# The first batch's xT is loaded by two requests of two row tiles each instead of one request of four

## The chip, the cores and the metric

The kernel runs on one core of one Trainium2 chip. The metric is the device time of one execution in microseconds (us). The kernel before takes 541.18 us (median of 3 runs, 540.99 to 541.9).

## What is computed

There are 16 independent batches, each a graph of 512 nodes with 256 features: x is 512 x 256 and adj is 512 x 512, all float32. Each batch goes through two residual blocks, a one-layer graph product and then a three-layer one:

```python
x = layernorm(x + adj @ (x @ W0 + b0) / rowsum(adj))
s = relu(adj @ (x @ W1) + b1)
s = relu(adj @ (s @ W2) + b2)
s = adj @ (s @ W3) + b3
out = layernorm(x + s)
```

No batch depends on another.

## The kernel before, in words

T = 4 row tiles of 128 nodes make up a batch, and KF = 2 tiles of 128 features. Every matrix that enters a product is split into a high and a low part (`_hi`, `_lo`): ScalarE (ACT) makes the high part with a copy, VectorE (DVE) or GpSimd (POOL) subtracts it from the full value for the low part. Each product is then three matmul passes on TensorE (PE): high times high, high times low, low times high (`three_passes`). The eight products of a batch are named p0 to p7: p0 is x @ W0 (it reads xT, x with its features on the partitions), p1 is adj @ h, which gives the first block's v1, p2 is the first product of the second block (it reads x1, the normalized v1), and so on.

The engines run queues written out by hand, and meet at counting semaphores. Batch 0 is `FIRST`, batch 1 is `second`; both have a start of their own, and from batch 2 on a loop does three batches a turn. The work of one batch is interleaved with that of the batch before and the one after.

Loads are issued by two engines, SyncE (SP) and ScalarE, each with a queue of its own: in the DMA rows q1 is SP's and q10 is ScalarE's. A load of a 128-partition tile reaches all 16 DMA engines, and each engine takes 8 partition rows of it. At the start of the kernel ScalarE issues, in this order, w0 (256 KB), the low half of batch 0's transposed adjacency (512 KB), batch 1's xT into the tile `y`, the low half of batch 1's adjacency into `adj_rows`, and batch 1's x into the tile `v2` (`v` in the rows). SP issues batch 0's xT (L220), the high half of batch 0's adjacency (L222), the biases b03 (L223, 256 KB), batch 0's x (L224), the high half of batch 1's adjacency (L225), W1 to W3 (L226) and the small biases (L227). Each of those without a size is 512 KB.

What reads them at the start, in queue order:

- ScalarE: `split_xT(FIRST, 0)` and `split_xT(FIRST, 1)` (high parts of row tiles 0, 1 and of 2, 3; L506, shown as L487), then the high parts of adjacency tiles 0 and 1, h tiles 0 and 1, adjacency tile 2, h tile 2, adjacency tile 3, h tile 3, and then batch 1's work.
- VectorE: w0's two parts, `split_xT(FIRST, 0)` and `(FIRST, 1)` (low parts), the low part of adjacency tile 0, h's low parts, then `norm1(FIRST)`.
- GpSimd: the low parts of adjacency tiles 1, 2 and 3 (L932), then `add_b0(FIRST)` (L914), which adds the bias to x_raw and gives xb; VectorE's v1 (L766) needs xb.
- TensorE: 18 warm-up matmuls on zeros, then `p0_first` (L308), which takes row tiles 0 to 3 in order. Tiles 0 and 1 need only the first half of xT, tiles 2 and 3 the second. Then come `p1_first` (which takes adjacency tile by adjacency tile for the first two outputs, and then outputs 2 and 3), `p0(second)`, and `p2_first`, whose four steps each wait for a tile of x1.

`norm1(FIRST)` and the normalization on ScalarE (`normalize_first`, L565 and L567) lead from v1 to x1; the low parts of x1 come from `split_x1_tile` (L939 on GpSimd, L693 on VectorE).

Of the kernel before, what the change touches and what calls it, by code (L numbers as in the profile page):

```python
# [12 lines left out]
DMA = 16  # L13
# [6 lines left out]
def build(nc, xT, x, adjT, adj, w0, w123, b03, b12, out):  # L20
    NB = x.shape[0]
    T = x.shape[2]
# [6 lines left out]
    with ExitStack() as ctx:  # L29
        def sb(name, shape, dt):  # L30
            return ctx.enter_context(nc.sbuf_tensor(name, shape, dt))

        def sem(name):
            return ctx.enter_context(nc.semaphore(name))


        xT_raw = sb("xT_raw", [P, T, F], F32)
# [57 lines left out]
        w123_loaded = sem("w123_loaded")  # L95
        b03_loaded = sem("b03_loaded")
        b12_loaded = sem("b12_loaded")
        xT1_loaded = sem("xT1_loaded")
        xT_loaded = sem("xT_loaded")
        x_loaded = sem("x_loaded")  # L100
# [65 lines left out]
        def at(batch, per, n):  # L166

            turn, r = batch
            return turn * (RING * per) + (r * per + n)

        def out_of(batch):

            return v1 if batch is LAST else y
# [38 lines left out]
        @block.sync  # L212
        def _(sp):

            sp.sem_inc(stored, DMA)
            def half_of(half, n):
                return slice(half * n // 2, (half + 1) * n // 2)

            sp.sem_inc(rows_ready, 2 * T)
            sp.dma_start(xT_raw[:, :, :], xT[0]).then_inc(xT_loaded, DMA)  # L220
            high = half_of(1, T)
            sp.dma_start(adj_raw[:, high, :], adjT[0, :, high, :]).then_inc(adj_loaded[1], DMA)  # L222
            sp.dma_start(b03_all[:, :], b03).then_inc(b03_loaded, DMA)  # L223
            sp.dma_start(x_raw[:, :, :], x[0]).then_inc(x_loaded, DMA)  # L224
            sp.dma_start(adj1_raw[:, high, :], adjT[1, :, high, :]).then_inc(adj1_loaded[1], DMA)  # L225
            sp.dma_start(w_raw[:, 1:4, :, :], w123).then_inc(w123_loaded, DMA)  # L226
            sp.dma_start(b12_col[:, 0:2 * KF], b12).then_inc(b12_loaded, DMA)  # L227

            def load(i, adj_free, rows_free):

                for half in range(2):
                    tiles = half_of(half, T)
                    adj_free(half)
                    sp.dma_start(adj_raw[:, tiles, :], adjT[i, :, tiles, :]).then_inc(adj_loaded[half], DMA)
                sp.wait_ge(xT_split, i * 2)
                sp.dma_start(xT_raw[:, :, :], xT[i]).then_inc(xT_loaded, DMA)
                sp.wait_ge(xb_ready, i * T)
                sp.dma_start(x_raw[:, :, :], x[i]).then_inc(x_loaded, DMA)
                rows_free()
                sp.dma_start(adj_rows[:, :, :], adj[i]).then_inc(rows_loaded, DMA)  # L240

            def third_adj_free(half):
                for k in range(half * T // 2, (half + 1) * T // 2):
                    sp.wait_ge(adj_tile_split[0][k], 1)

            def third_rows_free():
                for k in range(T):
                    sp.wait_ge(adj_tile_split[1][k], 1)

            load(2, third_adj_free, third_rows_free)  # L250
            sp.wait_ge(y_ready, T)
            sp.dma_start(out[0], y[:, :, :]).then_inc(stored, DMA)
            with sp.Fori(3, NB) as i:
                load(i, lambda half: sp.wait_ge(adj_split, (i - 3) * T + (half + 1) * T // 2),
                     lambda: sp.wait_ge(rows_ready, i * T))

                sp.wait_ge(y_ready, (i - 1) * T)
                sp.dma_start(out[i - 2], y[:, :, :]).then_inc(stored, DMA)
            sp.wait_ge(y_ready, (NB - 1) * T)
            sp.dma_start(out[NB - 2], y[:, :, :]).then_inc(stored, DMA)  # L260

            for j in range(T):
                sp.wait_ge(y_ready, (NB - 1) * T + j + 1)
                sp.dma_start(out[NB - 1, :, j, :], out_of(LAST)[:, j, :]).then_inc(stored, DMA)
            sp.wait_ge(stored, (1 + NB - 1 + T) * DMA)
# [219 lines left out]
        def _(act):  # L485
            def copy_hi(dst, src):
                return act.activation(dst, src, ACT.Copy)  # L487
# [6 lines left out]
            def split_xT(nxt, half):  # L494

                tiles = slice(half * T // 2, (half + 1) * T // 2)
                if nxt is second:
                    act.wait_ge(xT1_loaded, DMA)
                elif nxt is FIRST:
                    act.wait_ge(xT_loaded, DMA)  # L500
                else:
                    act.wait_ge(xT_loaded, at(nxt, DMA, 0))
                if nxt is not FIRST:
                    act.wait_ge(p0_done, at(nxt, T, 0))
                raw = xT1_raw if nxt is second else xT_raw
                copy_hi(xT_hi[:, tiles, :], raw[:, tiles, :]).then_inc(xT_hi_ready, 1)  # L506
# [105 lines left out]
            def step(new, last=False, ahead=True):  # L612
                old, nxt = before(new), before(new, -1)
                x3(old, 0)
                x3(old, 1)
                g(new, 0)
                if not last:
                    split_xT(nxt, 0)
                    split_xT(nxt, 1)
                g(new, 1)  # L620
                s3(old)
                x2(new, 0)
                x2(new, 1)
                if not last:
                    norm2(old, nxt=nxt)
                    h(nxt)
                    s2(new)
                    norm1(nxt, before(new, -2) if ahead else None)

            low = slice(0, T // 2)  # L630
# [5 lines left out]
            act.dma_start(adj1_raw[:, low, :], adjT[1, :, low, :]).then_inc(adj1_loaded[0], DMA)  # L636
            act.dma_start(x1_raw[:, :, :], x[1]).then_inc(x1_loaded, DMA)
            split_xT(FIRST, 0)
            split_xT(FIRST, 1)
            split_adj(FIRST, 0)  # L640
# [392 lines left out]
```

## Time and profile before

| | us |
|---|---|
| median of 3 runs | 541.18 (540.99 to 541.9) |
| the profiled execution | 541.69 |
| its span in the profile | 539.9 |
| PE busy | 531.2 (98% of the span) |
| DVE, ACT, POOL busy | 351.2, 312.4, 209.9 |

```profile
PE 531.2 (98%) x3829; PEld 496.8 (92%) x3829; DVE 351.2 (65%) x1059; ACT 312.4 (58%) x790; POOL 209.9 (39%) x227
...
PE   7899999999999999999999999999999999999996
...
PEclk9999999999999999999999999999999999999999
DMA  8530250703307051160602407043070612500002
```

These are the page's busy times and four of its lines in 40 slices of 13.5 us. A digit is the busy share of a slice in tenths. TensorE has a low digit only in the first slices and the last; the DMA engines are busiest in the first two. The span is the time between the first and the last instruction that the profile sees; the execution's own time lies 1.8 us above it.

### The profile page before, as it was taken

How to read it: one execution, taken by the hardware profiler on the slowest of the kernel's cores; microseconds unless marked ns; L12 is line 12 of the kernel's file. 1: busy time of each engine (PE TensorE's matmuls, PEld its weight loads, DVE VectorE, ACT ScalarE, POOL GpSimd, SP SyncE). 2: the span in 40 equal slices, each digit the busy share in tenths (PEclk: the TensorE clock that was granted, in tenths of full speed). 3: DMA queues.
4: the chain of work that ended last, by engine and by line, in shares of the span. 5: the costliest groups of instructions: out<-in, count | busy, mean ns of one | idle time of the engine just before them, and what ended most of it. 6: DMA issues, size and time to landing. Idle time of an engine off the chain costs nothing.

```text
span 539.9 us, 11045 instructions
## 1 busy us (share of the span) xinstructions
PE 531.2 (98%) x3829; PEld 496.8 (92%) x3829; DVE 351.2 (65%) x1059; ACT 312.4 (58%) x790; POOL 209.9 (39%) x227
## 2 busy tenths in 40 slices
PE   7899999999999999999999999999999999999996
PEld 7798989999899998989989899998999989899896
DVE  5684766747567475765757667485675757657546
ACT  5756655475665656655566655746655566554542
POOL 2667127081450906317072360904408063271100
PEclk9999999999999999999999999999999999999999
DMA  8530250703307051160602407043070612500002
GB/s 324 202 118 0 70 206 1 272 2 128 145 0 272 0 188 84 46 226 0 255 17 72 200 0 272 0 145 127 12 260 0 210 63 60 215 0 40 2 1 78
DMA packets 14566, 58.23 MB, mean 108 GB/s; under 512 B 1744, under 2 KB 2256, under 8 KB 12752
## 3 DMA queue, kind: packets, MB, share of 16 engines
q1 hardware_dynamic: 13824, 55.58, 28.2%
q10 hardware_dynamic: 720, 2.36, 1.2%
q8 instruction: 13, 0.21, 0.2%
q14 instruction: 9, 0.07, 0.0%
HBM read 49.55 MB, written 8.39 MB: 107 GB/s over the span
## 4 chain that ended last, share of the span: by engine, by line
PE 93%; DMA 2%; ACT 2%; DVE 1%; issue 0%; POOL 0%; SPq 0%; DVEq 0%; POOLq 0%
PE bank_a L186 16%; PE bank_a L187 16%; PE bank_a L188 16%; PE bank_b L186 15%; PE bank_b L188 14%; PE bank_b L187 14%; DMA x_raw<-in_x 2%; PE bank_b L278 1%; PE bank_b L279 1%; ACT x_hi L567 0%; ACT x L565 0%; DVE stats L820 0%; ACT adj_hi L487 0%; ACT std L607 0%; ACT h_hi L487 0%
## 5 line engine op out<-in xcount | busy, mean ns | idle before, releaser
L954 POOL TENSOR_TENSOR adj_lo<-adj_raw,adj_hi 128x512 fp32r<-128x512 f32 x56 | 70.7, 1296 | 261.8 <-ACT adj_hi L487 261.8
L693 DVE TENSOR_TENSOR x_lo<-bank_a,x_hi 128x512 fp32r<-128x512 f32 x62 | 42.8, 691 | 66.7 <-ACT bank_a L588 66.7
L186 PE MATMUL bank_b<-h_hi,adj_hi 128*128 128x256 f32 (+1 forms) x256 | 71.1, 278 | 0.4 <-POOL adj_lo L932 0.3
L555 ACT ACTIVATE std<-moments,eps_col 128x1 f32<-128x1 f32 x64 | 18.9, 295 | 90.5 <-DVE moments L790 90.5
L187 PE MATMUL bank_b<-h_lo,adj_hi 128*128 128x256 f32 (+1 forms) x256 | 70.8, 277 | 0.0
L188 PE MATMUL bank_b<-h_hi,adj_lo 128*128 128x256 f32 (+1 forms) x256 | 70.8, 276 | 0.0
L188 PE MATMUL bank_b<-s_hi,adj_lo 128*128 128x256 f32 x232 | 64.1, 276 | 0.0
L186 PE MATMUL bank_b<-s_hi,adj_hi 128*128 128x256 f32 x232 | 64.0, 276 | 0.0
L187 PE MATMUL bank_b<-s_lo,adj_hi 128*128 128x256 f32 x232 | 64.0, 276 | 0.0
L586 ACT ACTIVATE x_hi<-bank_a,b_col 128x512 fp32r<-128x512 f32 x62 | 42.3, 682 | 20.5 <-PE bank_a L188 19.6
L920 POOL TENSOR_TENSOR x1b<-x,b_all 128x256 f32<-128x256 f32 x64 | 46.0, 750 | 17.2 <-DVE x L777 17.2
L186 PE MATMUL bank_a<-adj_hi,s_hi 128*128 128x512 f32 x128 | 50.2, 392 | 0.0
L187 PE MATMUL bank_a<-adj_lo,s_hi 128*128 128x512 f32 x128 | 50.0, 391 | 0.0
L188 PE MATMUL bank_a<-adj_hi,s_lo 128*128 128x512 f32 x128 | 49.8, 389 | 0.0
L607 ACT ACTIVATE std<-moments,eps_col 128x1 f32<-128x1 f32 x64 | 18.9, 295 | 51.9 <-DVE moments L832 51.9
L186 PEld LDWEIGHTS bank_b<-h_hi,adj_hi 128*128 128x128 f32 x256 | 48.1, 188 | 0.9 <-issue 0.8
L188 PEld LDWEIGHTS bank_b<-h_hi,adj_lo 128*128 128x128 f32 x256 | 48.1, 188 | 0.0
L187 PEld LDWEIGHTS bank_b<-h_lo,adj_hi 128*128 128x128 f32 x256 | 48.1, 188 | 0.0
L693 DVE TENSOR_TENSOR g_lo<-bank_a,g_hi 128x512 fp32r<-128x512 f32 x30 | 20.7, 691 | 40.8 <-ACT g_hi L487 40.8
L186 PE MATMUL bank_a<-adj_hi,x_hi 128*128 128x512 f32 x120 | 46.7, 389 | 0.0
L187 PE MATMUL bank_a<-adj_lo,x_hi 128*128 128x512 f32 x120 | 46.7, 389 | 0.0
L188 PE MATMUL bank_a<-adj_hi,x_lo 128*128 128x512 f32 x120 | 46.7, 389 | 0.0
(150 smaller groups left out, 1721.2 us busy)
## 6 DMA issues: line engine op xcount, KB each, us to landing
adj_raw<-in_adjT SPq DMA_DIRECT2D x29, 512.0 KB, 5.5
adj_rows<-in_adj SPq DMA_DIRECT2D x14, 1024.0 KB, 9.4
xT_raw<-in_xT SPq DMA_DIRECT2D x15, 512.0 KB, 6.3
x_raw<-in_x SPq DMA_DIRECT2D x15, 512.0 KB, 7.3
out_y<-y SPq DMA_DIRECT2D x15, 512.0 KB, 2.9
w_raw<-in_w SPq DMA_DIRECT2D x1, 768.0 KB, 13.1
adj_raw<-in_adjT ACTq DMA_DIRECT2D x1, 512.0 KB, 6.1
y<-in_xT ACTq DMA_DIRECT2D x1, 512.0 KB, 7.9
```

The costliest lines, as they stand in the source:

```text
L186: pe.matmul(acc, st[0], mv[0], start=start, stop=False)
L187: pe.matmul(acc, st[0], mv[1], start=False, stop=False)
L188: return pe.matmul(acc, st[1], mv[0], start=False, stop=stop)
L278: pe.matmul(bank[j][:, 0:2 * F], hi, w_both[:, n, k, :, :], start=True, stop=False)
L279: mm = pe.matmul(bank[j][:, 0:F], lo, mv[0], start=False, stop=False)
L555: act.activation(std1[:, j:j + 1], moments1[:, j, 1:2], ACT.Sqrt, bias=eps_col[:, :]).then_inc(std1_ready, 1)
L586: act.activation(hi[:, f, :], bank[:, :], ACT.Relu, bias=bias[:, f:f + 1])
L607: act.activation(std2[:, j:j + 1], moments2[:, j, 1:2], ACT.Sqrt, bias=eps_col[:, :]).then_inc(std2_ready, 1)
L693: return dve.tensor_tensor(lo, full, hi.bitcast(F32), ALU.subtract)
L920: pool.tensor_tensor(x1b[:, slot(batch), j, :], x1[:, j, :], b3_all[:, :], ALU.add).then_inc(x1b_ready, 1)
L954: pool.tensor_tensor(adj_lo[:, s, k, :], adj_raw[:, k, :], adj_hi[:, s, k, :].bitcast(F32), ALU.subtract).then_inc(adj_split, 1)
```

## The change

The first request (xT of batch 0, all four row tiles, one semaphore) becomes two requests of two row tiles each, with a semaphore for each half. Each half is 256 KB; a partition row of it is 2 KB instead of 4 KB. ScalarE's `split_xT(FIRST, half)` waits for its own half. The semaphore of the later batches' xT starts one load lower. ScalarE and SP are the only queues whose text changes.

```diff
+        xT0_loaded = [sem(f"xT0_half{n}_loaded") for n in range(2)]
...
-            sp.dma_start(xT_raw[:, :, :], xT[0]).then_inc(xT_loaded, DMA)
-            high = half_of(1, T)
+            low, high = half_of(0, T), half_of(1, T)
+            sp.dma_start(xT_raw[:, low, :], xT[0, :, low, :]).then_inc(xT0_loaded[0], DMA)
+            sp.dma_start(xT_raw[:, high, :], xT[0, :, high, :]).then_inc(xT0_loaded[1], DMA)
...
                 elif nxt is FIRST:
-                    act.wait_ge(xT_loaded, DMA)
+                    act.wait_ge(xT0_loaded[half], DMA)
                 else:
-                    act.wait_ge(xT_loaded, at(nxt, DMA, 0))
+                    act.wait_ge(xT_loaded, at(nxt, DMA, -DMA))
```

On SyncE, at the start of the program, the kernel before has these requests (`b_all` is b03, `adj_rows` holds batch 1's adjacency here):

```order
L220 DMA xT_raw<-in_xT 128x1024
L222 DMA adj_raw<-in_adjT 128x1024
L223 DMA b_all<-in_b 128x512
L224 DMA x_raw<-in_x 128x1024
L225 DMA adj_rows<-in_adjT 128x1024
```

The changed kernel has these in the same place:

```order
L222 DMA xT_raw<-in_xT 128x512
L223 DMA xT_raw<-in_xT 128x512
L224 DMA adj_raw<-in_adjT 128x1024
L225 DMA b_all<-in_b 128x512
L226 DMA x_raw<-in_x 128x1024
L227 DMA adj_rows<-in_adjT 128x1024
```

One request of 1024 columns has become two of 512, and everything behind it is one request further back; x_raw is now the fifth in SyncE's queue. ScalarE's queue keeps its order: its two copies of xT stand ahead of the copies of the adjacency, the first waiting for the first half and the second for the second.

## Rows read from the trace of the kernel before

**Rows 1.** Busy time in stretches: us, PE, PEld, DVE, ACT, POOL, clock, DMA, GB/s
```profile
50.00:100.00 50.00, 50.00 (x392) 47.98 (x391) 33.77 (x103) 30.60 (x81) 19.87 (x23) 1.00 0.27 92
...
450.00:500.00 50.00, 50.00 (x376) 47.37 (x375) 35.43 (x113) 27.42 (x76) 15.12 (x17) 1.00 0.23 85
```

**Rows 2.** What PE waited for, whole span: us in total, times, longest
```profile
PE bank_b L314 <- ACT xT_hi L487: 1.1, 1, 1.1
PE bank_b L186 <- DVE x_lo L693: 1.0, 1, 1.0
```

**Rows 3.** The chain that ended last, in order of time: start us, us, what
```profile
2.27 11.12 DMA x_raw<-in_x
...
24.56 0.75 POOL x_lo L939
25.36 0.50 PE bank_b L186
```

**Rows 4.** The timeline's DMA requests: start us, us that issuing took, queue, line
```profile
0.88 0.39 SPq L220 DMA_DIRECT2D xT_raw<-in_xT  x1
1.17 0.45 ACTq L632 DMA_DIRECT2D adj_raw<-in_adjT  x1
1.32 0.43 SPq L222 DMA_DIRECT2D adj_raw<-in_adjT  x1
...
2.27 1.11 SPq L224 DMA_DIRECT2D x_raw<-in_x  x1
...
3.15 0.56 ACTq L637 DMA_DIRECT2D v<-in_x  x1
```

**Rows 5.** DMA issues before 3.25 us: count, KB, us from issue to landing
```profile
xT_raw<-in_xT SPq DMA_DIRECT2D x1, 512.0 KB, 4.6
adj_raw<-in_adjT ACTq DMA_DIRECT2D x1, 512.0 KB, 6.1
adj_raw<-in_adjT SPq DMA_DIRECT2D x1, 512.0 KB, 7.6
...
x_raw<-in_x SPq DMA_DIRECT2D x1, 512.0 KB, 11.1
v<-in_x ACTq DMA_DIRECT2D x1, 512.0 KB, 11.2
```

**Rows 6.** DMA queues, 3.75 to 4.5 us: packets, MB, share of 16 engines
```profile
q1 hardware_dynamic: 75, 0.31, 100.0%
q10 hardware_dynamic: 3, 0.00, 0.8%
```

**Rows 7.** DMA queues, 4.5 to 5 us
```profile
q1 hardware_dynamic: 43, 0.12, 59.2%
q10 hardware_dynamic: 24, 0.10, 47.7%
```

**Rows 8.** DMA queues, 5.5 to 6 us
```profile
q10 hardware_dynamic: 33, 0.14, 74.3%
q1 hardware_dynamic: 14, 0.06, 27.8%
```

**Rows 9.** DMA queues, 8 to 10 us, where SP's queue carries b03
```profile
q10 hardware_dynamic: 150, 0.55, 67.1%
q1 hardware_dynamic: 145, 0.27, 34.6%
```

**Rows 10.** DMA queues, 0 to 13.4 us
```profile
q10 hardware_dynamic: 701, 2.35, 49.8%
```

**Rows 11.** DMA queues, 12.8 to 13.4 us
```profile
q10 hardware_dynamic: 30, 0.12, 50.6%
```

**Rows 12.** ScalarE in the timeline: start us, us, line, what [idle before <- releaser]
```profile
5.51 1.15 ACT L487 ACTIVATE xT_hi<-xT_raw 128x512 fp32r<-128x512 f32 x2 [2.37 <-DMA xT_raw<-in_xT]
7.28 1.16 ACT L487 ACTIVATE adj_hi<-adj_raw 128x512 fp32r<-128x512 f32 x2 [0.61 <-DMA adj_raw<-in_adjT]
```

**Rows 13.** GpSimd in the timeline
```profile
8.51 3.79 POOL L932 TENSOR_TENSOR adj_lo<-adj_raw,adj_hi 128x512 fp32r<-128x512 f32 x3 [8.06 <-ACT adj_hi L487]
13.53 2.15 POOL L914 TENSOR_TENSOR xb<-x_raw,b_all 128x256 f32<-128x256 f32 x3 [1.23 <-DMA x_raw<-in_x]
```

**Rows 14.** TensorE in the timeline: `p1_first` at its fourth adjacency tile
```profile
12.45 0.36 PE L186 MATMUL bank_b<-h_hi,adj_hi 128*128 128x258 f32 x1 [0.29 <-POOL adj_lo L932]
```

## The prediction

> **What bounds the kernel now.** I read the busy times by stretch first. From 50 to 500 us TensorE is busy in all 50.00 us of each 50 us stretch [rows 1] (the first and the last of nine stretches). Whatever happens there, nothing that this change touches can be late or early. What is left is the start, and a change there moves the end one for one: TensorE's work behind the start has no idle time to take up a delay or to fill with a gain.
>
> The list of TensorE's waits comes next. Two in the start matter: 1.1 us before the first p0 matmul, for the copy of xT, and 1.0 us in `p2_first`, for a low part of x1 [rows 2]. Only the first has to do with xT; the question is whether it is on the path, and the chain of waits says no. It runs over the load of x_raw, which is issued at 2.27 us and takes 11.12 us, up to 13.39; from there over xb, v1, the moments and ScalarE's normalization to the low part of x1's last tile (24.56 us, 0.75 us) and to the matmul at 25.36 us [rows 3]. GpSimd had been idle for 1.23 us when x_raw landed [rows 13]. TensorE waits again after its p0 and p1 work: a p0 that starts sooner only makes those later waits longer, as long as x_raw does not land sooner.
>
> The third view is the DMA queues, since x_raw's landing is a matter of their order. From 8 to 10 us they move 0.55 + 0.27 = 0.82 MB, 0.41 MB per us [rows 9], and that is the pace of the whole stretch up to x_raw: the landing is set by bytes ahead of it, not by its issue.
>
> **The first half and p0.** xT's request goes out at 0.88 us [rows 4] and lands 4.6 us later, at 5.48 [rows 5]; ScalarE copies from 5.51 on, after 2.37 us idle [rows 12]. Between 3.75 and 4.5 us the SP queue has the engines for itself [rows 6]: a half of 256 KB (0.262 MB) takes 0.262/0.41 = 0.64 us less than the whole, so it should land about 0.6 us sooner, near 4.9, and perhaps nearer 4.6. `p0_first` then starts about as much sooner. Worth on the path: 0, because x_raw's chain covers it. If this cover were gone it would be worth at most the 1.1 us of [rows 2].
>
> **The second half lands late.** The DMA queues show in which order packets are served. From 3.75 to 4.5 us xT alone is served, though the low adjacency half had been issued on ScalarE's queue at 1.17 us, before SP's next request at 1.32 [rows 4, 6]. Then the low adjacency half comes (24 packets from 4.5 to 5, xT's last 43 beside it) [rows 7], and only from about 5.7 does SP's second request begin (14 packets by 6.0) [rows 8]. So requests get served about in the order of issue over both queues, and SP's second request stands behind most of ScalarE's second one. From then on the queues alternate packet by packet: from 8 to 10 us SP's 2 KB rows of b03 get 145 packets against 150 packets of 4 KB, equal in number with half the bytes [rows 9]. In the changed kernel SP's second request is the second half of xT. It takes the high adjacency half's old place, moved 0.64 us forward by the shorter first half, and its 8 rows per engine alternate with 4 KB rows. A row of 4 KB takes 4096 x 16 / 0.41 MB per us = 0.16 us on an engine, one of 2 KB 0.08. The high adjacency half landed at 1.32 + 7.6 = 8.92 [rows 4, 5]; take off 0.64, and 8 x 0.08 = 0.64 for the shorter rows: about 7.6 us for xT's second half, 2.1 us after the whole xT lands now.
>
> What is queued behind that wait: ScalarE's second copy of xT, and behind it the copies of the adjacency, which start at 7.28 now [rows 12]. They would start at 7.6 plus one copy (1.15/2 = 0.6), near 8.2: 0.9 to 1.0 us late. GpSimd's three adjacency subtractions follow from 9.5 instead of 8.51 and end at 13.3 instead of 12.30 [rows 13]; TensorE's fourth adjacency step moves from 12.45 [rows 14] to about 13.4. All of this stays just ahead of xb, for GpSimd had 1.23 us of idle time before x_raw. Cost on the path: 0, with some 0.3 to 0.6 us of that cover left. If the second half came 0.5 us later than I say, this chain would take over from x_raw's.
>
> **x_raw lands later.** This is the term that counts. Bytes ahead of x_raw in SP's queue are the same as before, but there are 8 more rows per engine, and in packet-by-packet alternation each lets a row of ScalarE's queue pass. ScalarE's queue is nearly through when x_raw lands: batch 1's x (the `v` row) is issued at 3.15 and lands 11.2 later, at 14.35 [rows 4, 5], and five transfers of 128 rows and 16 small completion packets each are 720 packets, of which 701 were done by 13.4 [rows 10]. So the eight rows can let pass only what is left. Two readings of it: on the last engine 14.35 - 13.39 = 0.96 us of alternation, of which ScalarE's share is half, 0.48 us (3 rows of 0.16); over all engines the 0.12 MB after 12.8 us [rows 11], 0.29 us. (12.8 because xT's last packets went before 5.0 [rows 7] and its landing was at 5.48, so x_raw's last packets left about 0.5 us before 13.39.) I take 0.4 us, nearer to the last engine, which is the one that the semaphore waits for. Bounds: 0 if the second half is served right behind the first, since bytes and alternation then stay as they are up to there; 0.96 if all of batch 1's x and as much of SP's next load went ahead.
>
> **One more issue on SP.** Another request takes about 0.43 us to issue [rows 4], so x_raw's request starts at 2.7 instead of 2.27. It has over 9 us in the queue, with b03 ahead of it; cost 0. All other edits are semaphore counts; cost 0, as no instruction is added on the computing engines.
>
> **Sum.** 0 (p0 sooner) + 0 (adjacency later, covered) + 0.4 (x_raw) = +0.4 us. The profiled execution took 541.69 us, with 1.8 us around its span of 539.9, and would take 542.1; it lies 0.5 us above the median of the runs, 541.18, from which I forecast: 541.6 us.
>
> The Trainium skill, page "DMA: Bandwidth & Descriptors", section "Queues, rings and completion order", says that an engine drains a whole packet of some 9 to 17 descriptors from one queue before it turns to the other. Its rule would make the queues take turns by whole requests here. Rows 10 speak against it: when x_raw had landed, batch 1's x was nearly through, where by turns it would only be starting.
>
> **Rivals.**
> A, turns by whole requests. The place is the same, x_raw. Every request of SP is then followed by a whole one of ScalarE's, and the one request more lets all of batch 1's x (512 KB, 0.524/0.41 = 1.28 us) pass: +1.28, 542.5 us, slower. For it: the pure stretches of rows 6 and 7. Against it: rows 9, and the 701 packets of rows 10. This is the result of the page's rule named above.
>
> B, engines left idle: slower as well. The low adjacency half was issued at 1.17 us and had hardly a packet before 4.5 [rows 6, 7]. If that is no matter of order but the time at which its rows are there to be served, the shorter first half leaves the engines idle until then. This costs up to the whole 0.64 us, on top of the 0.4: +1.04, 542.2 us, and up to 542.7 if the later requests come at such intervals too. It decides from 1.08 us on. For it: the high adjacency half first shows at 5.7, 4 us after its issue, and the gaps between first packets are about 1.1 us. Against it: each first packet comes just where the other queue's request is nearly done, and no stretch after 3.75 us shows spare share.
>
> C, x_raw does not move: the halves are served back to back, or the engines' uneven pace swallows the three rows. 541.2 us. Also the case of a change that does what it says and is hidden at both ends.
>
> D, faster. The earlier p0 would have to reach the end, and that needs the 1.0 us wait in `p2_first` [rows 2] to fall with it. Only an earlier x_raw does that; were its chain gone, at most 1.1 us, 540.1. I see nothing for it but that the page attributes waits by inference.
>
> **How the numbers follow.** Forecast 0.52, A 0.04, B 0.20, C 0.21, D 0.03. Of this kernel 0.2% (1.08 us) is about what a measurement can tell from no change. Beyond it on the slow side lie A and half of B, with a little of the forecast's upper end (0.02): 0.16. On the fast side only D: 0.03. The rest, 0.81, is within. The range takes in the forecast (541.2 to 542.1 by its bounds), C with 0.3 us of scatter as in the runs of before, and B's first value: 540.9 to 542.7.
>
> **What the profile after would show.** Right: the first p0 matmul at least 0.5 us sooner; xT's second copy on ScalarE at 7.3 to 8 us, with TensorE waiting for it inside p0; the adjacency copies near 8.2; GpSimd's xb at 13.8 to 14.1, and still with idle time before it released by x_raw; the matmul of 25.36 [rows 3] at 25.7 to 25.9; from 50 us on no wait. Wrong: xT's second copy right after the first (then C), DMA shares that fall below full between 4 and 5 us (then B), xb later than 14.4 (A or B), or GpSimd's adjacency work ending after x_raw's landing, which would make the late second half itself the bound.

## The result and the profile after

The changed kernel takes 543.09 us (median of 6 runs, 542.82 to 543.29), the kernel before 541.13 in the same comparison (540.67 to 541.9). The ratio is 1.0033 with a 95% interval of 1.0024 to 1.0043: slower by 1.96 us, clear of noise. I had forecast 541.6, in a range up to 542.7. A second comparison gave 543.07 against 541.27, 1.0032 (1.0020 to 1.0045).

The profiled execution took 543.0 us with a span of 541.2; that of before took 541.69 with a span of 539.9. The spans are 1.3 us apart, less than the medians, because this execution of the kernel before was 0.5 us slower than its median. The chain of waits of the changed kernel (start, us, what) still runs over x_raw:

```profile
3.02 11.70 DMA x_raw<-in_x
...
25.89 0.76 POOL x_lo L941
26.64 0.04 issue
26.69 0.50 PE bank_b L187
```

Against [rows 3], x_raw lands at 14.72 instead of 13.39 and the matmul of 25.36 starts at 26.69: both 1.33 us later. The last matmul starts at 536.39 instead of 535.08, 1.31 us, so the end follows x_raw within 0.02 us. TensorE's waits over the whole span (us in total, times, longest) are:

```profile
PE bank_b L316 <- ACT xT_hi L489: 1.3, 2, 1.0
...
PE bank_b L187 <- DVE x_lo L695: 1.0, 1, 1.0
```

The first wait of [rows 2] has become two. p0 starts 0.6 us sooner, at 5.65 us, and then waits again for the second half of xT, which lands late. The DMA issues before 3.25 us of the changed kernel (count, KB, median us from issue to landing) show it together with x_raw's own landing:

```profile
xT_raw<-in_xT SPq DMA_DIRECT2D x2, 256.0 KB, 5.5
...
x_raw<-in_x SPq DMA_DIRECT2D x1, 512.0 KB, 11.7
```

The 5.5 is the middle of 4.0 and 7.0: the first half lands at 4.88, the second at 8.32, where the whole xT landed at 5.48 before. ScalarE and GpSimd in the timeline, against [rows 12, 13]:

```profile
4.88 0.63 ACT L489 ACTIVATE xT_hi<-xT_raw 128x512 fp32r<-128x512 f32 x1 [1.73 <-DMA xT_raw<-in_xT]
8.36 0.63 ACT L489 ACTIVATE xT_hi<-xT_raw 128x512 fp32r<-128x512 f32 x1 [2.85 <-DMA xT_raw<-in_xT]
8.89 1.14 ACT L489 ACTIVATE adj_hi<-adj_raw 128x512 fp32r<-128x512 f32 x2
```
```profile
10.11 4.01 POOL L934 TENSOR_TENSOR adj_lo<-adj_raw,adj_hi 128x512 fp32r<-128x512 f32 x3 [9.65 <-ACT adj_hi L489]
14.86 2.16 POOL L916 TENSOR_TENSOR xb<-x_raw,b_all 128x256 f32<-128x256 f32 x3 [0.74 <-DMA x_raw<-in_x]
```

The whole adjacency work is 1.6 to 1.8 us late, and still ends 0.74 us before xb may start. It is x_raw that ends the wait, as in the kernel before.

A part of x_raw's 1.33 us is seen in the DMA totals of the first 7 us, before and after:

```profile
DMA packets 523, 1.68 MB, mean 241 GB/s; under 512 B 48, under 2 KB 48, under 8 KB 523
```
```profile
DMA packets 580, 1.43 MB, mean 204 GB/s; under 512 B 49, under 2 KB 49, under 8 KB 580
```

More packets, and 0.25 MB less: at 0.41 MB per us that is 0.6 us lost for good. In these two profiles most of it lies between 5 and 7 us, where the two queues move 0.26 and then 0.33 MB in a microsecond, against 0.40 and 0.40 before (the sum of both rows in each stretch):

```profile
q10 hardware_dynamic: 49, 0.19, 72.2%
q1 hardware_dynamic: 34, 0.07, 17.8%
```
```profile
q10 hardware_dynamic: 83, 0.34, 89.3%
q1 hardware_dynamic: 16, 0.06, 14.0%
```

These are the rows of the stretch 5 to 6 us (packets, MB, share), the changed kernel first. A 4 KB row of ScalarE's queue (q10) takes longer here: 72.2% of 16 us over 49 packets is 0.24 us, against 0.17 before. From 7 us on both kernels run at 0.41 again.

The second profile of the changed kernel (e11) loses as much by 7 us, but from 4 us on. Its rows of 4 to 5 us:

```profile
q10 hardware_dynamic: 59, 0.24, 83.8%
q1 hardware_dynamic: 3, 0.00, 0.2%
```

The first half was through at about 4.0 us, and SyncE's queue (q1) is next served at 5.2. ScalarE's queue has the engines alone in between and moves 0.24 MB in this microsecond, where the kernel before moved 0.42 with both. The first profile has the same gap from 4.4 to 5.2 us. So a part of the loss comes before any row of the second half is served.

### The profile page after: what moved, and what is told of

It reads as the page before. It is cut to its first block, busy times and chain, and to the rows that moved or that the text cites. A ratio compares the mean times of both kernels' runs of the same rounds, so it can differ in the third digit from the quotient of the medians.

```text
span 541.2 us, 11046 instructions
## 1 busy us (share of the span) xinstructions
PE 532.2 (98%) x3829; PEld 497.7 (92%) x3829; DVE 351.2 (65%) x1059; ACT 312.4 (58%) x790; POOL 210.3 (39%) x227
## 4 chain that ended last, share of the span: by engine, by line
PE 92%; DVE 2%; DMA 2%; ACT 2%; issue 1%; SPq 0%; POOL 0%; DVEq 0%; POOLq 0%
PE bank_a L187 16%; PE bank_a L188 16%; PE bank_a L189 16%; PE bank_b L187 14%; PE bank_b L189 14%; PE bank_b L188 14%; DMA x_raw<-in_x 2%; PE bank_b L280 1%; PE bank_b L281 1%; ACT x_hi L569 0%; ACT x L567 0%; DVE x L779 0%; DVE stats L822 0%; ACT adj_hi L489 0%; ACT std L609 0%
```

## The experiments

All are compared with the kernel before on the same chips; its median (19 runs beside e1 to e4, 28 beside the others) was 541.27 to 541.30. "Landing" is x_raw's in the profiled execution, one for each kernel; a star marks where another load's chain set the time.

| kernel | median us | ratio, 95% interval | landing | MB by 7 us |
|---|---|---|---|---|
| before (two profiles) | 541.27, 541.14 | 0.9997 (0.9988 to 1.0006) | 13.39, 13.94 | 1.68, 1.66 |
| changed (two profiles) | 543.09, 543.07 | 1.0033, 1.0032 | 14.72, 14.62 | 1.43, 1.44 |
| e1 first copy waits for both halves | 544.16 | 1.0051 (1.0037 to 1.0065) | 14.9* | 1.43 |
| e2 halves by partitions | 544.47 | 1.0060 (1.0047 to 1.0074) | 15.9* | 1.41 |
| e3 tiny request second | 542.58 | 1.0025 (1.0016 to 1.0035) | 15.09 | 1.31 |
| e7 tiny request ahead of x_raw | 542.55 | 1.0022 (1.0013 to 1.0031) | 14.26 | 1.68 |
| e12 tiny request behind x_raw | 541.35 | 1.0002 (0.9993 to 1.0011) | 13.4 | 1.74 |
| e9 one request, 2 KB rows | 542.16 | 1.0018 (1.0009 to 1.0027) | 14.13 | 1.55 |
| e5 before, x1 last | 540.86 | 0.9993 (0.9984 to 1.0002) | 12.57 | 1.70 |
| e6 changed, x1 last | 542.15 | 1.0018 (1.0009 to 1.0027) | 13.51* | 1.45 |
| e8 second half on ScalarE's queue | 543.01 | 1.0030 (1.0018 to 1.0042) | 12.5* | 1.58 |
| e10 try at a faster kernel | 541.54 | 1.0005 (0.9996 to 1.0014) | 11.2* | 1.70 |

My theory after the result was that x_raw's landing sets the time and the DMA queues delay it, by rows that let the other queue pass and by a dead time at their start (a stretch in which the queues move less than they could). Its rival was that the late second half of xT itself sets the time.

**e1: both halves awaited by the first copy.**

```diff
-                    act.wait_ge(xT0_loaded[half], DMA)
+                    act.wait_ge(xT0_loaded[0], DMA)
+                    act.wait_ge(xT0_loaded[1], DMA)
```

> The changed kernel, but ScalarE's first copy of xT waits for both halves. The requests are the same. Theory Q (the DMA queues make x_raw land late, and nothing else counts): p0 starts near 9.0 instead of 5.65 us, x_raw still lands near 14.7, and the time is that of the changed kernel, 543.1 within 0.3. Theory W (the late second half holds up ScalarE's copies and the adjacency chain sets the time): that chain comes another half microsecond later, 543.6.

Neither number came: 544.16. With p0 at 9.29, the adjacency chain did take over, and by more than I had said. GpSimd's rows:

```profile
13.21 2.58 POOL L935 TENSOR_TENSOR adj_lo<-adj_raw,adj_hi 128x512 fp32r<-128x512 f32 x2 [0.99 <-ACT adj_hi L489]
15.74 1.90 POOL L917 TENSOR_TENSOR xb<-x_raw,b_all 128x256 f32<-128x256 f32 x2
```

xb starts with no idle time before it: its queue, not x_raw, was last. The adjacency copies wait in ScalarE's queue behind h's, and these for p0, whose matmuls ran at the lower rate after 3.9 us without work (last section). So the early start of the first half is worth about 1.1 us against this version; it only covers what the split itself makes late. In the changed kernel the late second half is not the bound: the work that it holds up still ends 0.74 us before xb may start (0.59 in e11).

**e2: two requests cut by partitions.**

```diff
-            sp.dma_start(xT_raw[:, low, :], xT[0, :, low, :]).then_inc(xT0_loaded[0], DMA)
-            sp.dma_start(xT_raw[:, high, :], xT[0, :, high, :]).then_inc(xT0_loaded[1], DMA)
+            sp.dma_start(xT_raw[0:P // 2, :, :], xT[0, 0:P // 2]).then_inc(xT0_loaded[0], DMA)
+            sp.dma_start(xT_raw[P // 2:P, :, :], xT[0, P // 2:P]).then_inc(xT0_loaded[1], DMA)
```

> xT comes in two requests, cut by partitions (64 partitions each, rows of 4 KB, 4 rows per engine and request), and ScalarE waits for both. The rows per engine are 8 as in the kernel before; only the request is one more. If it is the number of rows that counts (each lets a row of ScalarE's queue pass): x_raw at 13.4, 541.1 us. If it is the request itself (dead time of about 0.6 us between 5 and 7 us in the changed kernel): x_raw near 14.0, 541.8 us. If both halves of my sum are tied to the second request standing behind the low adjacency half: 542 to 543.

It was the slowest of all. With rows of 4 KB and no more rows than before, the queues moved only 0.3 MB per us from 6 to 8 us. xT's second part landed at 9.21 and x_raw at 15.9, later than any of the three cases expected. Since ScalarE waits for both parts as in e1, p0 and the adjacency chain were late too and set the time, so this run gives no price for one more request by itself. It does say that rows of full length do not save a cut load. That the place of the second part behind the other queue's load is what hurts in both cuts is likely, but not shown by this run.

**e3, e7, e12: one small request in three places.** In each, this line of the kernel before is moved up from the end of the first loads: in e3 behind xT's, in e7 ahead of x_raw's, in e12 behind it.

```diff
+            sp.dma_start(b12_col[:, 0:2 * KF], b12).then_inc(b12_loaded, DMA)
```

> The kernel before, with the small request b12 (128 rows of 16 bytes) moved from the end of SP's queue to the place right behind xT. One request and 8 rows per engine more stand ahead of x_raw, and next to no bytes. Row theory: the rows of the other queue that pass bring x_raw 0.3 to 0.5 us later, 541.5. Row and dead time together: x_raw at 14.3 to 14.7, 542.1 to 543.1. Byte theory (only bytes count): 541.1.

> The kernel before, with the small request b12 moved to the place right ahead of x_raw in SP's queue (fourth; in the run before it stood second and cost 1.4 us by the medians). Row theory: its 8 rows per engine let ScalarE's last rows pass, 0.3 to 0.5 us, 541.6. Dead time theory: an extra request costs 0.6 to 1.1 us only while the queues are starting up, so nothing of that shows here. If every request costs the same anywhere in the queue: 542.6 as for the second place.

> The kernel before, with the small request b12 moved to the place right behind x_raw in SP's queue. As second request it cost 1.4 us and right ahead of x_raw 1.3 (medians). Behind x_raw it can only delay later loads, which nothing waits for: 541.2 us, no change. If an additional request early in the program costs wherever it stands, 542 or more.

A load of 2 KB costs 1.3 us of the whole kernel when it stands ahead of x_raw, in either place, and nothing behind it. That refutes the byte theory. In e3 the small request is served in the queues' start, and the engines stand partly idle. The rows of 5 to 7 us:

```profile
q10 hardware_dynamic: 77, 0.27, 58.7%
q1 hardware_dynamic: 39, 0.00, 0.9%
```

That is 0.28 MB in 2 us, at a share of 60%, where the kernel before moves 0.80. But it is not only the start that is sensitive: e7 lost nothing by 7 us, and here is its stretch of 10 to 12 us, where the small request is served:

```profile
q10 hardware_dynamic: 160, 0.59, 79.4%
q1 hardware_dynamic: 164, 0.06, 10.5%
```

0.65 MB in 2 us instead of 0.82, in 324 packets: the two queues take turns packet by packet, and the 16 byte rows of the one do not leave their time to the other. This is 0.4 us. The rest of e7's 0.87 us by landings (14.26 against 13.39) fits rows of ScalarE's queue that went ahead of x_raw: batch 1's x, 0.96 us behind x_raw before, now lands at 3.04 + 10.4 = 13.4, ahead of it.

**e9: short rows without a second request.** The first batch's xT is stored as two halves in DRAM, and one request fetches both.

```diff
-            sp.dma_start(xT_raw[:, :, :], xT[0]).then_inc(xT_loaded, DMA)
+            sp.dma_start(xT_raw[:, :, :].rearrange("p (h t) f -> p h (t f)", h=2),
+                         xT0.rearrange("h p t f -> p h (t f)")).then_inc(xT_loaded, DMA)
```

> The kernel before, with batch 0's xT stored in DRAM as two halves one behind the other, so that its one request has 16 rows of 2 KB per engine instead of 8 of 4 KB; the bytes, the number of requests and the waits are those of before. This parts rows from requests. If the change's loss (1.3 us by x_raw's landing) comes with the rows that have to be served: the DMA queues fall behind between 5 and 7 us as in the changed kernel (1.43 MB by 7 us against 1.69) and x_raw lands near 14.5, 542.5 to 543 us. If it comes with the request and its place behind the low adjacency half: x_raw near 13.4 to 13.9, 541.3 us.

The median, 542.16, is 0.9 us above the kernel before, half of the change's 1.8 in these comparisons. By 7 us the queues have moved 1.55 MB, half of the shortfall. So the shorter rows alone, with the same bytes, the same request and the same wait, cost about half (0.5 to 1.5 us by the interval); the other half is left for the second request, by difference.

The loss does not come while the short rows are served. From 3.5 to 4 us they have the engines alone, at the full pace; from 5 to 6 us xT is through and ScalarE's 4 KB rows are served nearly alone (the rows of e9 in these two stretches):

```profile
q1 hardware_dynamic: 95, 0.19, 104.3%
```
```profile
q10 hardware_dynamic: 54, 0.22, 87.1%
q1 hardware_dynamic: 4, 0.02, 4.0%
```

This is the gap of e11 again, here from about 4.5 to 5.8 us: SyncE's first request is through, its second not yet served, and ScalarE's rows take 0.26 us each. The kernel before has such a gap too (4.9 to 5.6 us in the first profile, 4.6 to 5.4 in the second, e4). In its first profile ScalarE's queue kept the full pace in it, 0.20 MB from 5 to 5.5 us; in e4 it did not:

```profile
q10 hardware_dynamic: 34, 0.14, 99.3%
```

The gap is longer in the changed kernel (0.8 and 1.2 us) and in e9 (1.3) than in the kernel before (0.7 and 0.8). I read a part of the loss from this; no run changes the gap by itself.

**e5 and e6: batch 1's x moved out of ScalarE's queue**, in the kernel before and in the changed one.

```diff
-            act.dma_start(x1_raw[:, :, :], x[1]).then_inc(x1_loaded, DMA)
...
+            sp.dma_start(x1_raw[:, :, :], x[1]).then_inc(x1_loaded, DMA)
```

> The kernel before, with batch 1's x (512 KB, ScalarE's fifth request) moved to the end of SP's queue. In the first profile five of its eight rows per engine went ahead of x_raw. Row theory: x_raw lands 5 x 0.16 = 0.8 us sooner, and since the end follows x_raw one for one (+0.55 and +0.5 in the second profile of before), the time falls by 0.8 us, to 540.3. If another chain is right behind x_raw's, less of it is seen. If the number of requests in the first 7 us is what counts, x_raw gains less.

> The changed kernel with the same move of batch 1's x. Row theory: now all eight rows of it went ahead of x_raw, so x_raw gains 1.28 us, from 14.7 to 13.4, but GpSimd's adjacency work, which ended 0.74 us before x_raw's landing, then sets the time: a gain of 0.7, 542.4 us. If rows that pass were the whole of the change's cost, this kernel and the one before with the same move would be equal but for that chain; if the dead time is a part of its own, x_raw stays 0.6 us later than there.

x_raw gained 0.82 us in the one (12.57, by 0.8 as forecast) and 1.21 in the other. The difference, 0.39 us, looks like the term of 0.4 of my sum, but it hangs on which profiles are taken: against the second ones (13.94 and 14.62) the gains are 1.37 and 1.11, and the difference is -0.26. So the size of that term is not shown. Between e5 and e6, where these rows are out of the way, 0.94 us remain. 0.6 of them are the 0.25 MB by 7 us (1.70 and 1.45). The other 0.3 I can't place: it is smaller than the landing's own scatter. In e6 x_raw is no longer the bound; the chain runs over the high half of the adjacency:

```profile
1.80 8.79 DMA adj_raw<-in_adjT
...
11.32 2.24 POOL adj_lo L934 x2
13.56 0.26 issue
13.82 1.20 POOL xb L916
```

So the loads behind the split are late as well, and would cap what a better order could bring. By the median e5 is 0.4 us faster than before, half of what was expected, with an interval (0.9984 to 1.0002) that just includes no change. e6 came at 542.15, near the 542.4 expected.

**e8: the second half on ScalarE's queue**, ahead of the low adjacency half.

```diff
-            sp.dma_start(xT_raw[:, high, :], xT[0, :, high, :]).then_inc(xT0_loaded[1], DMA)
...
+            act.dma_start(xT_raw[:, T // 2:T, :], xT[0, :, T // 2:T, :]).then_inc(xT0_loaded[1], DMA)
```

> The changed kernel with the second half of xT issued by ScalarE, between w0 and the low adjacency half, instead of by SP. The number of requests and of rows is that of the changed kernel; the second half no longer stands behind the low adjacency half. Row theory: SP's queue has 8 rows fewer ahead of x_raw than in the changed kernel, so no row of ScalarE's passes in their place: x_raw near 13.4 if there is no dead time, near 14 to 14.4 if there is. Second half: lands near 5.5 to 6 instead of 8.3 us. Time 541.2 without, 541.8 to 542.2 with dead time.

The second half now landed at 1.17 + 4.3 = 5.5 us, and x_raw at 2.27 + 10.2 = 12.5. x_raw was sooner than I had expected (13.4 to 14.4), with 256 KB less ahead of it in SyncE's queue. In exchange the low adjacency half landed at 1.65 + 7.5 = 9.2 instead of 1.17 + 6.1 = 7.3, for it has both halves of xT ahead of it, and its chain set the time: 543.01, above both of my cases. SyncE's second request was served from about 4.6 us on here, against 5.2 to 5.8 in all the kernels where a load of 512 KB stands second in ScalarE's queue and 128 partitions are loaded at a time: its start is tied to what the other queue has to serve, and not to its own issue at 1.32 us alone.

**e10: a try at a faster kernel.** As e5, and b03 moved to ScalarE's queue ahead of the low half of batch 1's adjacency.

```diff
-            sp.dma_start(b03_all[:, :], b03).then_inc(b03_loaded, DMA)
...
+            act.dma_start(b03_all[:, :], b03).then_inc(b03_loaded, DMA)
             act.dma_start(adj1_raw[:, low, :], adjT[1, :, low, :]).then_inc(adj1_loaded[0], DMA)
```

> A try at a faster kernel, from the one before: batch 1's x moved to the end of SP's queue, and the biases b03 moved from SP's queue to ScalarE's, ahead of the low half of batch 1's adjacency. x_raw is then third on SP, b03 fourth on ScalarE; both should land near 11 to 11.5 us instead of 13.4 and 10.8. GpSimd's adjacency work, which ends at 12.3, then sets the start of xb: 12.35 against 13.53, so 1.0 to 1.2 us less than before, 540.1 to 540.3. Against it: the low half of batch 1's adjacency lands later (near 13), which ScalarE needs ahead of the first square root at 15.58; there is room for it.

x_raw landed at 1.80 + 9.4 = 11.2, as forecast. The low half of batch 1's adjacency, for which I had said near 13 and room enough, landed at 14.89. The chain:

```profile
3.04 11.85 DMA adj_rows<-in_adjT
...
15.44 0.29 ACT std L555
```

ScalarE waits in order for batch 1's adjacency until 14.89 and takes the first square root at 15.44, 0.14 us sooner than before (15.58). 541.54 instead of 540.1 to 540.3: no gain.

**e4 and e11: both kernels again.**

> The kernel before once more, to see how far its own times and its landing of x_raw differ from run to run: its runs so far spread over 1.2 us (540.67 to 541.9), those of the changed kernel over 0.5. If x_raw's landing sets the time, this profile's span minus the first one's (539.9) is x_raw's landing minus 13.39, and the shift of the median by 1.96 us against 1.33 in the profiled landings is the profiled run of before having been a late one.

> The changed kernel once more, beside the others on one chip: median 543.1 within 0.3. The landing of x_raw (14.72 in the first profile) tells how it scatters; the two profiles of the kernel before had 13.39 and 13.94. If the span minus x_raw's landing is 526.5 again, the end follows x_raw one for one here too.

The second profile of the kernel before landed x_raw at 13.94 with a span of 540.4, the first at 13.39 with 539.9: the same 526.5 us from landing to end, which the changed kernel (541.2 - 14.72), e3, e5, e7 and e12 show too. e9 and e11 need 526.0. About half of these 0.5 us lies around TensorE's first matmul of adj_hi with s_hi. In the first profile of before:

```profile
38.39 0.28 PE L188 MATMUL bank_a<-h_hi,adj_lo 128*128 128x258 f32 x1
38.66 0.50 PE L186 MATMUL bank_a<-adj_hi,s_hi 128*128 128x512 f32 x1
39.00 0.40 PE L187 MATMUL bank_a<-adj_lo,s_hi 128*128 128x512 f32 x1
39.24 0.40 PE L188 MATMUL bank_a<-adj_hi,s_lo 128*128 128x512 f32 x1
```

and in e11:

```profile
39.43 0.28 PE L189 MATMUL bank_a<-h_hi,adj_lo 128*128 128x258 f32 x1
39.55 0.40 PE L187 MATMUL bank_a<-adj_hi,s_hi 128*128 128x512 f32 x1
39.79 0.40 PE L188 MATMUL bank_a<-adj_lo,s_hi 128*128 128x512 f32 x1
40.02 0.39 PE L189 MATMUL bank_a<-adj_hi,s_lo 128*128 128x512 f32 x1
```

From the last matmul of the one phase to the third of the next it is 0.85 us in the first and 0.59 in the second: 0.26 us of short stalls that an execution has or hasn't. In the first profile of the changed kernel the chain of waits runs over VectorE's s_lo at this place. So the time of one execution scatters by at least two things, x_raw's landing (half a microsecond in before) and this.

Both profiled executions of the kernel before were late ones, 0.5 and 1.05 us above their medians (541.69 against 541.18, 542.19 against 541.14); those of the changed kernel lay 0.1 and 0.6 below theirs (543.0 against 543.09, 542.44 against 543.07). That is why the medians are 1.8 to 1.96 apart and the profiled spans 1.3. If a typical execution of before also ends 526.5 us after the landing, with 1.8 us around the span, it lands x_raw at 541.2 - 1.8 - 526.5 = 12.9: an estimate, no such execution was traced.

## Why the prediction was wrong, point by point

**The bound.** Right. x_raw's load and its chain set the time, TensorE's first wait was not on the path, and the end moved by what x_raw moved.

**The first half.** Right in size: forecast 0.6 us sooner, landed at 4.88 instead of 5.48, and p0 started 0.64 us sooner (in the second profiles ScalarE's copy starts at 4.39 against 5.22). It was worth 0 on the path, as said.

**The second half.** Right in kind, short in size: forecast near 7.6, measured 8.32; adjacency copies forecast near 8.2, measured 8.89. I had moved the second request of SyncE's queue forward by 0.64 us with the end of the first; it was first served at 5.2 us, against 5.6 and 5.4 in the two profiles of the kernel before. The cover left, forecast 0.3 to 0.6, measured 0.74, came near by two errors that offset each other: the adjacency was later than forecast, and so was x_raw.

**x_raw.** This is the step that failed, and in its premise: "0.41 MB per us [rows 9], and that is the pace of the whole stretch up to x_raw". I let the shorter rows and the additional request change only the order in which bytes are served. They also change how many are served: 0.25 MB less by 7 us, 0.6 us. The pace was 0.26 MB per us from 5 to 6 us in the first profile and 0.24 from 4 to 5 in the second.

The term that I did work out, rows of ScalarE's queue that pass, was 0.4. Its direction shows: batch 1's x landed 0.96 us after x_raw before, and 0.6 us ahead of it in the changed kernel. Its size does not, as e5 and e6 give 0.39 or -0.26 by the profiles taken; that the first of them is the forecast number is luck. 0.4 + 0.6 would be 1.0 of the 1.33 us by landings, and about half of the 1.96 us by medians; the rest has no term of its own. By e9's median, half of the total falls to the short rows and the rest to the second request.

**The rivals.** B (0.20) came nearest, and nearer than its own words: a term of up to 0.64 us on top of the 0.4, 542.2 to 542.7. It was wrong on which request is late. It had the low adjacency half's rows only ready at about 4.5 us; in the changed kernel ScalarE's queue (q10) moves 34 packets from 4 to 4.5 us, against 3 from 3.75 to 4.5 before [rows 6], so they were ready when the first half was through. The DMA totals of 4 to 4.5 us, changed kernel:

```profile
DMA packets 75, 0.20 MB, mean 401 GB/s; under 512 B 11, under 2 KB 11, under 8 KB 75
```

The request that was not served in time was SyncE's second one: nothing of it before 5.2 us, though the first was through at 4.4 us (4.0 in e11) and it had been issued at 1.32. Its sign, shares below full between 4 and 5 us, is weak in the first profile (92% from 4.5 to 5) and plain in e11 (84%). From 5.5 to 6 us of the first profile the share is 62%. So engines left idle are a part of it, and rows of ScalarE's queue that take longer another (0.24 us each from 5 to 6 us, 0.23 in e11 from 4 to 5, against 0.17 before).

A (turns by whole requests) is out: batch 1's x lands at 2.61 + 11.5 = 14.11, only 0.6 us before x_raw and not a whole request of 1.28 us, and from 6 to 7 us the two queues get about as many packets, though those of q1 are shorter (again the changed kernel):

```profile
DMA packets 132, 0.33 MB, mean 330 GB/s; under 512 B 14, under 2 KB 14, under 8 KB 132
...
q10 hardware_dynamic: 56, 0.18, 51.0%
q1 hardware_dynamic: 76, 0.15, 42.6%
```

C and D did not happen.

**The range.** I took the median of before as the base, and the profiled landing of x_raw as the place of the change. The profiled execution was a late one, by 0.5 us, so the landing that I started from was probably too late by about as much, and against a typical run the change is worth more. Nothing in my range stood for that.

Open: why ScalarE's queue does not keep the full pace when it has the engines alone near 5 us, why SyncE's second request is served so late, and what short rows and one more request add to both. The runs show less than the full pace after 2 KB rows (e9), with 16 byte rows (e3, e7) and with 64-partition requests (e2), and for a shorter time also in the kernel before (0.29 MB from 5 to 6 us in e4).

## What to carry to other kernels

Before a load is cut in two, look up what the second request will stand behind: here it was not served before 5.2 us, beside the other queue's 512 KB, landed 2.8 us after the uncut load had, and pushed every later load of the start. Count the rows of a request, not only its bytes: a 2 KB load of 128 rows ahead of the bounding load cost 1.3 us, behind it nothing that could be measured. A wait that is removed from TensorE is worth nothing while another load bounds the start; find that load first, and move what it does not need behind it. Even that brought only 0.4 us here (e5), not clear of noise.

## What the runs showed of the hardware that I had not expected

Two queues with work take turns row by row, whatever the rows' size (160 against 164 packets in e7, 150 against 145 in [rows 9]). With 2 KB rows on one side the pace is kept, 0.82 MB in 2 us [rows 9]; with 16 byte rows it is not, 0.65 MB (e7).

One queue alone can move the full pace (q1 with 2 KB rows in e9, 0.19 MB in half a microsecond; q10 with 4 KB rows in the first profile of the kernel before, 0.20) or much less (q10 in e4, 0.14; in e11, 0.24 in a whole microsecond). What decides is open.

TensorE's level did not always show in the granted clock. The timeline of TensorE in the second profile of the kernel before (e4; start us, us, line, what), at four of p0's matmuls of 256 columns:

```profile
6.56 0.63 PE L317 MATMUL bank_b<-w_both,xT_hi 128*128 128x256 f32 x2
6.99 0.63 PE L320 MATMUL bank_b<-w_both,xT_lo 128*128 128x256 f32 x2
```

The stretch of 6.00 to 10.80 us in the same profile (stretch, its length, TensorE's busy time and count, granted clock, DMA share, GB/s):

```profile
6.00:10.80 4.80, 4.80 (x24) 1.00 1.03 412
```

And two such pairs in the first profile of the kernel before:

```profile
7.50 0.39 PE L317 MATMUL bank_b<-w_both,xT_hi 128*128 128x256 f32 x2
7.72 0.39 PE L320 MATMUL bank_b<-w_both,xT_lo 128*128 128x256 f32 x2
```

Two matmuls start every 0.43 us in the one, 0.21 us for 256 columns, which is the level of 1.2 GHz, and every 0.22 to 0.23 from 7.26 us on in the other, the level of 2.4 GHz. The granted clock reads 1.00 for both. The slow pace lasts to 9.97 us. TensorE had been idle for 0.59 us before p0 there, and for 1.13 in the fast one, so the idle time alone does not tell which comes. It cost nothing there, as x_raw came later. In e1, where TensorE had been idle for 3.9 us, p0 was slow as well and it did cost.
